# A gated cross-attention block with an expert layer: rounded queries and keys taken off ScalarE, and the last ten residuals summed by TensorE

## The chip, the cores and the metric

One Trainium2 chip, one core of it. The metric is the device time of one execution in microseconds (us); the figure given is the median of several runs. The engines are called TensorE (PE), VectorE (DVE), ScalarE (ACT), GpSimd (POOL) and SyncE (SP), as in the profile.

## The reference, cut to what matters

```python
# x, ctx: (128 batches, 64 tokens, 128 features), float32; 16 heads of 8 features
def attention(q, k, v):
    qh, kh, vh = heads(q @ W_q + b_q), heads(k @ W_k + b_k), heads(v @ W_v + b_v)
    probs = softmax(qh @ kh.T / sqrt(8))
    return merge(probs @ vh) @ W_o + b_o
x = x + tanh(g_xattn) * attention(layernorm(x), ctx, ctx)
# 8 experts 128 -> 256 -> 128, one per token, chosen by the largest gate
xn = layernorm(x)
gates = softmax((xn @ w_red) @ normalized(wg).T)
e, score = argmax(gates), max(gates)
x = x + tanh(g_ffn) * score * (gelu(xn @ W1[e] + b1[e]) @ W2[e] + b2[e])
```

## The kernel before, in words

The 8192 tokens are 64 units of 128 tokens (two batches each), and four units make a chunk: 16 chunks of 512 tokens. The attention is a pipeline over 76 slots (`SLOTS`), the outer `for k in range(SLOTS)` loop of every engine; chunk `s = k // 4` and position `j = k % 4`. In slot k TensorE computes the first scores of unit k-4 (`scores1`, called by `peaks`), the second scores of unit k-10 (`scores2`), the values of unit k-11 and the output projection of unit k-12 (`values`). Beside these, each slot holds a quarter of the preparation of chunk s: position 0 turns the normalized rows and the context, position 1 projects the keys, position 2 the queries, position 3 the values.

**Two passes over the scores.** The softmax needs the largest score of each row first. `scores1` computes scores from bfloat16 queries `qb` and keys `kb`, the latter spread by DMA into the block-diagonal tile `Kd`; VectorE reduces them to maxima (L1054, in two halves, `mxa_ok` and `mx_ok`). `scores2` computes them again in float32 from `Qd` (spread by DMA from `Qf`) and `kT`, with the maxima subtracted by a product of `MD` and `usel` (L1192). ScalarE takes the exponentials in two halves (L631, L633); the first waits for `mxa_ok` of the unit that `scores1` handled in this slot, the second for `mx_ok`. The next slot's `scores2` waits for the second exponential. So each slot closes a loop: TensorE scores2, scores1; VectorE first half of the maxima; ScalarE two exponentials; TensorE again.

**Keys and queries.** In position 1 ScalarE writes `kb` (L599, from PSUM, bias added, rounded to bfloat16) and then `kT` (L606, two instructions: float32, one for the even and one for the odd rows, each masked by `par`). TensorE's values product (L1428) overwrites the same bank `m1` and waits for both. SyncE's queue waits for `kb_ok` and issues four DMAs from `kb` to `Kd` (L325), then waits for `qf_ok` and issues four from `Qf` to `Qd` (L332), then the weight loads and the loads of later chunks. `scores1` of unit 4s runs in slot 4s+4 and waits for all four `Kd` DMAs of chunk s (L1220): three slots after `kb` is written. In position 2 ScalarE writes `qb` (L662, bfloat16) and `Qf` (L665, float32) from the same bank.

**GpSimd's queue.** For each chunk c from 2 on, `norm(c)` (called with s = c-1) computes the reciprocal deviation by a power (L380, when VectorE has the variance, L769, in slot 4(c-1)+1), three small instructions (L384, L385, L389), and then four times a normalized unit `xn` (L404) and the copy of x with the output bias (L408). TensorE turns `xn` in slot 4c. From s = 7 on GpSimd also issues the indirect DMAs that scatter finished rows to the experts' lists (`send`, L439); the table `sends` gives for each s how many stand before `norm` and how many behind it: three before at s = 8, 9, 11 and 12, four at s = 14, two at s = 15.

**Residuals.** Each unit's projected output is added to x by VectorE: `residual(k)`, L1042, `XR = out * tg + XR` over 137 columns (128 features, 8 gate logits, 1 mean). From slot 66 (`APART`) on, the output stands in a bank of its own (`m1`) and the residual is VectorE's last act for the unit in the slot; TensorE's next projection waits for it (`x1_ok`). ScalarE's `squares` (L561) read the sum a slot later. The routing (`route_peak` and what follows) runs on VectorE at slots set by `route_slots`.

**The expert layer** follows: 71 tiles of 128 rows, its first pieces inside slots 70 to 75. ScalarE loads the table of Gelu in slot 73 (L699).

## Time and profile before

| | |
|---|---|
| median of 3 runs | 354.69 us (352.94 to 355.47) |
| the profiled execution | 356.73 us |
| its span, first to last instruction | 355.0 us |
| mean granted TensorE clock | 0.968 of full speed |
| busy: PE, DVE, ACT, POOL | 300.8, 285.4, 252.8, 231.1 us |
| attention slots with scores2 | 32.55 to 240.3 us |
| expert tiles alone | from 246 us |

The page and the timeline are of the one profiled execution. A group of instructions is told by its line, the engine and the tiles it writes and reads. "[0.28 <-ACT PT L633]" behind an instruction is the idle time of its engine just before it and what ended it.

### The profile page before, as it was taken

How to read it: one execution, taken by the hardware profiler on the slowest of the kernel's cores; microseconds unless marked ns; L12 is line 12 of the kernel's file. 1: busy time of each engine (PE TensorE's matmuls, PEld its weight loads, DVE VectorE, ACT ScalarE, POOL GpSimd, SP SyncE). 2: the span in 40 equal slices, each digit the busy share in tenths (PEclk: the TensorE clock that was granted, in tenths of full speed). 3: DMA queues.
4: the chain of work that ended last, by engine and by line, in shares of the span. 5: the costliest groups of instructions: out<-in, count | busy, mean ns of one | idle time of the engine just before them, and what ended most of it. 6: DMA issues, size and time to landing. Idle time of an engine off the chain costs nothing.

```text
span 355.0 us, 16204 instructions
## 1 busy us (share of the span) xinstructions
PE 300.8 (85%) x6014; PEld 223.6 (63%) x6014; DVE 285.4 (80%) x1025; ACT 252.8 (71%) x651; POOL 231.1 (65%) x372
## 2 busy tenths in 40 slices
PE   2968899998999898999898787667988999999940
PEld 1535666665675665666665655456777999999830
DVE  7777999899998999999999799988777666666610
ACT  3766799989999889998998795767443555555410
POOL 6493654184498885798188643277777777777771
PEclk9998999999999999999999898999999999999985
DMA  5354345344313322423121112421135543433110
GB/s 118 84 172 151 92 144 175 86 142 104 96 58 122 123 67 78 143 67 118 54 74 59 67 61 75 118 71 60 49 94 141 139 118 109 110 101 101 57 41 0
DMA packets 47160, 34.05 MB, mean 96 GB/s; under 512 B 9800, under 2 KB 42955, under 8 KB 47083
## 3 DMA queue, kind: packets, MB, share of 16 engines
q1 hardware_dynamic: 42440, 23.90, 23.9%
q0 software_dynamic: 4352, 9.00, 7.6%
q8 instruction: 49, 0.80, 1.0%
q14 instruction: 27, 0.22, 0.2%
q10 hardware_dynamic: 292, 0.13, 0.1%
HBM read 17.13 MB, written 10.04 MB: 77 GB/s over the span
## 4 chain that ended last, share of the span: by engine, by line
PE 43%; DVE 22%; ACT 17%; issue 10%; POOL 3%; DMA 2%; ACTq 1%; POOLq 0%; DVEq 0%; SPq 0%
PE m L1366 10%; PE sc L1338 8%; DVE mx L1054 6%; ACT PT L633 4%; PE sc L1199 4%; ACT PT L631 3%; ACT dev L561 3%; PE sc L1209 3%; PE sc L1192 3%; PE m L1428 3%; DVE TV L1063 2%; PE m L1363 2%; PE pv L1274 2%; PE sc L1326 2%; DVE NV L1074 2%
## 5 line engine op out<-in xcount | busy, mean ns | idle before, releaser
L1054 DVE TENSOR_REDUCE mx<-sc 128x8 f32<-128x512 f32 x128 | 81.9, 682 | 14.0 <-PE sc L1209 13.7
L439 POOL DMA_INDIRECT records<-XR,pos x64 | 62.7, 979 | 35.2 <-DVE XR L926 17.5
L498 POOL DMA_INDIRECT out<-fo,rr x71 | 70.3, 990 | 21.5 <-issue 20.0
L631 ACT ACTIVATE PT<-sc 128x512 f32<-128x512 f32 x64 | 38.2, 597 | 19.1 <-issue 13.2
L380 POOL TENSOR_TENSOR rstd<-ve,mhalf 128x4 f32<-128x4 f32 x16 | 16.7, 1041 | 53.3 <-DVE ve L769 53.2
L1366 PE MATMUL m<-w,fgT 128*128 x280 | 49.0, 298 | 0.1
L1033 DVE SCALAR_TENSOR_TENSOR fo<-m,rr 128x128 f32<-128x128 f32 x70 | 24.5, 350 | 27.2 <-PE m L1366 26.9
L1338 PE MATMUL sc<-fxT,w1s 128*128 128x128 f32 x276 | 43.3, 279 | 3.1 <-DVE w1s L1025 2.7
L1274 PE MATMUL pv<-PT,V 128*32 128x64 f32 x2048 | 42.9, 223 | 1.1 <-DVE NV L1074 0.7
L614 ACT ACTIVATE fxT<-sc 128x128 f32<-128x128 f32 x69 | 19.2, 278 | 30.2 <-PE sc L1326 30.2
L1199 PE MATMUL sc<-Qd,kT 32*128 32x128 f32 x1024 | 40.3, 274 | 0.0
L1338 PEld LDWEIGHTS sc<-fxT,w1s 128*128 128x128 f32 x276 | 36.2, 191 | 5.6 <-ACT fxT L614 2.7
L620 ACT ACTIVATE fgT<-sc 128x256 f32<-128x256 f32 x69 | 26.5, 384 | 18.1 <-PE sc L1338 17.8
L633 ACT ACTIVATE PT<-sc 128x512 f32<-128x512 f32 x64 | 38.3, 598 | 0.0
L1274 PEld LDWEIGHTS pv<-PT,V 128*32 128x32 f32 x2048 | 32.3, 110 | 9.3 <-issue 2.0
L1366 PEld LDWEIGHTS m<-w,fgT 128*128 128x128 f32 x280 | 36.6, 190 | 2.2 <-issue 0.2
L1192 PEld LDWEIGHTS sc<-MD,usel 32*128 32x128 bf16 x256 | 6.4, 91 | 47.9 <-ACT PT L633 45.6
L1192 PE MATMUL sc<-MD,usel 32*128 32x256 bf16 x256 | 18.5, 280 | 21.2 <-ACT PT L633 18.9
L1199 PEld LDWEIGHTS sc<-Qd,kT 32*128 32x128 f32 x1024 | 35.1, 189 | 0.0
L1063 DVE STREAM_TRANSPOSE TV<-pv 128x256 f32<-128x256 f32 x64 | 28.2, 440 | 0.6 <-PE pv L1274 0.4
L1009 DVE TENSOR_SCALAR fx<-rr 128x127 f32<-128x127 f32 x71 | 27.9, 392 | 0.1
L561 ACT ACTIVATE dev<-XR 128x128 f32<-128x128 f32 x64 | 26.1, 407 | 0.5 <-DVE XR L1042 0.5
(229 smaller groups left out, 695.8 us busy)
## 6 DMA issues: line engine op xcount, KB each, us to landing
rr<-records SPq DMA_DIRECT2D x71, 72.0 KB, 2.0
XC<-in_x SPq DMA_DIRECT2D x16, 256.0 KB, 4.4
C<-in_ctx SPq DMA_DIRECT2D x16, 256.0 KB
Qd<-Qf SPq DMA_DIRECT2D x64, 64.0 KB
Kd<-kb SPq DMA_DIRECT2D x64, 32.0 KB, 2.2
w<-in_L_ffn_W SPq DMA_DIRECT2D x16, 128.0 KB, 3.4
out<-fo,rr POOLq DMA_INDIRECT x71, 2.3
w1l<-in_L_ffn_W SPq DMA_DIRECT2D x8, 128.0 KB, 3.9
```

The costliest lines, as they stand in the source:

```text
L439: nc.gpsimd.indirect_dma_start(out=records, out_offset=bass.IndirectOffsetOnAxis(ap=pos[:, u:u + 1], axis=0), in_=XR[:, u, :], in_offset=N ...
L498: nc.gpsimd.indirect_dma_start(out=out_rows, out_offset=bass.IndirectOffsetOnAxis(ap=rr[q][:, R_ID:R_ID + 1].bitcast(U32), axis=0), in_=fo ...
L561: nc.scalar.activation(dev2[:, :], X[:, n, :], ACT.Square, bias=XR[:, n, R_MEAN:R_MEAN + 1], scale=-1.0, accum_out=gsq[c % 2][:, u:u + 1]) ...
L631: nc.scalar.activation(pt[:, 0:2], sc[:, 0:2, 256:512], ACT.Exp)
L633: nc.scalar.activation(pt[:, 2:4], sc[:, 2:4, 256:512], ACT.Exp).then_inc(pt_ok, 1)
L1054: nc.vector.tensor_reduce(mx[c % 2][:, t:t + 2, HI * u:HI * u + HI], sc[:, t:t + 2, 0:256].rearrange("p t (i k) -> p t i k", i=HI), AX_X, ...
L1063: nc.vector.transpose(TV[:, :, :].rearrange("p a r -> p (a r)"), pv[:, 0:2 * P]).then_inc(tv_ok, 1)
L1192: nc.tensor.matmul(sc[:, t, 256:512].rearrange("p (b i q) -> p i b q", b=2, i=2), usel[r, u, :, :].rearrange("r l k -> r (l k)"), MD[c % 2 ...
L1199: m = nc.tensor.matmul(sc[:, t, 256 + P * b:256 + P * b + P].rearrange("p (i q) -> p i q", i=2), kT[c % 3][r, u, b, :, :].rearrange("r l k ...
L1274: last = nc.tensor.matmul(pv[32 * t:32 * t + 32, P * b:P * b + P].rearrange("p (h i q) -> p i h q", h=2, i=2)[:, i], vf[:, at:at + 32], PT ...
L1338: i = nc.tensor.matmul(hidden(k)[:, P * m:P * m + P], w1s[p][:, P * m:P * m + P], fxT[p][:, :], start=True, stop=True, skip_group_check=True)
L1366: i = nc.tensor.matmul(o, fgT[p][:, m, :], w2[:, bass.ds(e, 1), m, :].rearrange("p o c -> p (o c)"), start=False, stop=(m == HH - 1), skip ...
```

## The change

On ScalarE the bfloat16 queries go: `qb` becomes a view of the upper halves of the float32 `Qf` (every second bfloat16 element, cut rather than rounded), and `Qf` gets a second buffer. For chunks 2 to 15 the bfloat16 keys are no longer written by ScalarE: GpSimd adds the two halves of `kT` into `kb`, in `norm` behind `deviation`, ahead of the `xn` of the next chunk. TensorE's values product waits for `kT` alone. In the last ten slots TensorE adds x to the projected output in PSUM by a product with the identity, and ScalarE copies the sum out; `wox` is multiplied by `tg` once, so the other 54 residuals on VectorE become plain additions.

```diff
-        Qf = sb("Qf", [P, CT])
-        qb = [sb(f"qb{i}", [P, CT], BF16) for i in range(2)]
+        Qf = [sb(f"Qf{i}", [P, CT]) for i in range(2)]
+        qb = [q[:, :].bitcast(BF16).rearrange("p (t two) -> p t two", two=2)[:, :, 1] for q in Qf]
...
+            def rounded_keys(s):
+                pool.wait_ge(kT_ok, s + 1)
+                pool.wait_ge(kd_in[(s - 1) % 2], 16 * HI * ((s - 1) // 2 + 1))
+                k = kT[s % 3][:, :, :, :, :].rearrange("r u b p k -> r (u b) p k")
+                nc.gpsimd.tensor_tensor(kb[:, :].rearrange("r (a k) -> r a k", k=S), k[:, :, 0, :], k[:, :, 1, :],
+                                        ALU.add).then_inc(kb_ok, 1)
             def norm(c):
                 deviation(c)
+                if c >= 3:
+                    rounded_keys(c - 1)
...
                     norm(s + 1)
+                if s + 1 == NC:
+                    rounded_keys(s)
...
-                nc.scalar.activation(wox[:, D:DX], pv[:, 0:NX], ACT.Copy).then_inc(wox_ok, 1)
+                act.wait_ge(tg_ok, 1)
+                nc.scalar.activation(wox[:, D:DX], pv[:, 0:NX], ACT.Copy, scale=tg[:, 0:1])
+                nc.scalar.activation(wox[:, 0:D], wox[:, 0:D], ACT.Copy, scale=tg[:, 0:1]).then_inc(wox_ok, 1)
+            def residual(n):
+                act.wait_ge(pv_ps, pv_turn(n + LAGO))
+                act.wait_ge(x1_ok, n)
+                nc.scalar.activation(XR[:, n, 0:DX], attn_out(n + LAGO), ACT.Copy).then_inc(x1_ok, 1)
...
                 if j == 1 and 1 <= s < NC:
-                    keys(s)
+                    if s == 1:
+                        keys(s)
+                    else:
+                        act.wait_ge(k_ps, s + 1)
                     keys_turned(s)
                 if j == 2 and s < NC:
                     act.wait_ge(q_ps, s + 1)
                     if s >= 2:
                         act.wait_ge(s1_ps, CU * (s - 1))
-                    nc.scalar.activation(qb[s % 2][:, :], m0[:, :], ACT.Identity, bias=b16[:, 0:1], scale=ISC).then_inc(qb_ok, 1)
-                    if s >= 1:
-                        act.wait_ge(qd_in[(s - 1) % 3], 16 * HI * ((s - 1) // 3 + 1))
-                    nc.scalar.activation(Qf[:, :], m0[:, :], ACT.Identity, bias=b16[:, 0:1], scale=ISC).then_inc(qf_ok, 1)
+                        act.wait_ge(qd_in[(s - 2) % 3], 16 * HI * ((s - 2) // 3 + 1))
+                    nc.scalar.activation(Qf[s % 2][:, :], m0[:, :], ACT.Identity, bias=b16[:, 0:1], scale=ISC).then_inc(qf_ok, 1)
...
+                if APART <= k:
+                    residual(k - LAGO)
...
-                    nc.vector.scalar_tensor_tensor(out=XR[:, n, 0:DX], in0=attn_out(k), scalar=tg[:, 0:1], in1=XR[:, n, 0:DX],
-                                                   op0=ALU.mult, op1=ALU.add).then_inc(x1_ok, 1)
+                    nc.vector.tensor_tensor(XR[:, n, 0:DX], attn_out(k), XR[:, n, 0:DX], ALU.add).then_inc(x1_ok, 1)
...
-                if k >= APART:
-                    residual(k)
...
-                        pe.wait_ge(qb_ok, c + 1)
+                        pe.wait_ge(qf_ok, c + 1)
...
+                    if k >= APART:
+                        pe.wait_ge(xb_ok, no // CU + 1)
+                        pe.wait_ge(lgx_ok, no // CU + 1)
+                        nc.tensor.matmul(attn_out(k), ident[:, :], XR[:, no, 0:DX], start=True, stop=False, skip_group_check=True)
...
-                    pe.wait_ge(kb_ok, s + 1)
+                    if s < 2:
+                        pe.wait_ge(kb_ok, s + 1)
                     pe.wait_ge(kT_ok, s + 1)
```

## Rows read from the trace of the kernel before

**Rows 1.** The page, part 1: busy time of each engine, its share, its instructions.

```profile
PE 300.8 (85%) x6014; PEld 223.6 (63%) x6014; DVE 285.4 (80%) x1025; ACT 252.8 (71%) x651; POOL 231.1 (65%) x372
```

**Rows 2.** The page, part 4: the chain that ended last, by engine.

```profile
PE 43%; DVE 22%; ACT 17%; issue 10%; POOL 3%; DMA 2%; ACTq 1%; POOLq 0%; DVEq 0%; SPq 0%
```

**Rows 3.** Timeline, 136 to 144 us, PE and ACT: start us, duration us, engine, line.

```profile
136.88 0.29 PE L1192 MATMUL sc<-MD,usel 32*128 32x256 bf16 x4 [0.17 <-ACT PT L633]
...
137.33 1.44 ACT L606 ACTIVATE kT<-m,bkp,par 128x512 f32<-128x512 f32 x2
...
138.83 1.12 PE L1421 MATMUL m<-xT,wqp 128*128 128x512 f32 x2
...
139.04 0.60 ACT L631 ACTIVATE PT<-sc 128x512 f32<-128x512 f32 x1
...
140.18 0.29 PE L1192 MATMUL sc<-MD,usel 32*128 32x256 bf16 x4 [0.22 <-ACT PT L633]
...
143.21 0.29 PE L1192 MATMUL sc<-MD,usel 32*128 32x256 bf16 x4
```

**Rows 4.** Lines by form: line, engine, shapes, count | busy us, mean ns | idle.

```profile
L1209 PEld LDWEIGHTS sc<-Kd,qb 32*64 32x64 bf16 x512 | 8.0, 102 | 8.7 <-DVE mx L1054 1.3 <-issue 0.2
...
L423 POOL TENSOR_TENSOR w<-w,w1l 128x512 f32<-128x512 f32 x4 | 5.0, 1284 | 0.0
...
L599 ACT ACTIVATE kb<-m,b 128x512 bf16<-128x512 f32 x16 | 11.0, 686 | 2.0 <-PE m L1316 2.0
...
L1042 DVE SCALAR_TENSOR_TENSOR XR<-m,tg,XR 128x137 f32<-128x137 f32 x10 | 3.2, 324 | 0.0
```

**Rows 5.** Timeline, 137 to 142 us, POOL and SP's queue.

```profile
137.31 1.04 POOL L380 TENSOR_TENSOR rstd<-ve,mhalf 128x4 f32<-128x4 f32 x1 [5.41 <-DVE ve L769]
...
137.46 2.39 SPq L325 DMA_DIRECT2D Kd<-kb  x4
...
138.86 0.19 POOL L389 TENSOR_TENSOR std<-ve,rstd 128x4 f32<-128x4 f32 x1
```

**Rows 6.** The tile Kd: issue ns min/median/max and landing us, whole run; landing, 137 to 141 us.

```profile
L325 SPq DMA_DIRECT2D Kd<-kb x64: 459/592/1567, 12.2 to 208.0; - x64
...
DMA to landing us min/median/max: 1.6/2.2/3.6
...
DMA to landing us min/median/max: 1.7/1.8/1.8
```

**Rows 7.** Timeline, 143 to 146 us: the slot that first uses these keys.

```profile
143.88 0.32 PE L1209 MATMUL sc<-Kd,qb 32*64 32x256 bf16 x8
...
144.29 1.29 DVE L1054 TENSOR_REDUCE mx<-sc 128x8 f32<-128x512 f32 x2 [0.26 <-PE sc L1209]
...
145.32 0.58 ACT L631 ACTIVATE PT<-sc 128x512 f32<-128x512 f32 x1
```

**Rows 8.** Timeline, 111 to 118, 151 to 157 and 191 to 199 us: three other chunks.

```profile
111.83 1.06 POOL L380 TENSOR_TENSOR rstd<-ve,mhalf 128x4 f32<-128x4 f32 x1
...
116.94 0.32 PE L1209 MATMUL sc<-Kd,qb 32*64 32x256 bf16 x8
...
117.99 0.68 DVE L1054 TENSOR_REDUCE mx<-sc 128x8 f32<-128x512 f32 x1
...
151.38 1.05 POOL L380 TENSOR_TENSOR rstd<-ve,mhalf 128x4 f32<-128x4 f32 x1
...
156.48 0.32 PE L1209 MATMUL sc<-Kd,qb 32*64 32x256 bf16 x8
...
191.61 1.06 POOL L380 TENSOR_TENSOR rstd<-ve,mhalf 128x4 f32<-128x4 f32 x1
...
198.75 0.32 PE L1209 MATMUL sc<-Kd,qb 32*64 32x256 bf16 x8
```

**Rows 9.** Windows: stretch us, span, busy us of PE, PEld, DVE, ACT, POOL, PEclk, DMA.

```profile
200.00:203.00 3.00, 3.00 (x30) 2.62 (x30) 1.90 (x7) 2.71 (x7) 1.58 (x2) 0.52 0.19 64
```

**Rows 10.** Timeline, 241 to 243 us, ACT: the table load of the last exponentials.

```profile
241.71 1.28 ACT L699 ACT_TABLE_LOAD   x1
```

More of the change, by code:

```diff
@@ L189, in gated_block @@
         q_ps, k_ps, v_ps = (sem(n) for n in ("q_ps", "k_ps", "v_ps"))
-        qb_ok, qf_ok, kb_ok, kT_ok, v_ok = (sem(n) for n in ("qb_ok", "qf_ok", "kb_ok", "kT_ok", "v_ok"))
+        qf_ok, kb_ok, kT_ok, v_ok = (sem(n) for n in ("qf_ok", "kb_ok", "kT_ok", "v_ok"))
         kd_in = [sem(f"kd_in{i}") for i in range(2)]
@@ L331, in _ @@
                 for i in range(HI):
-                    sp.dma_start(Qd[s % 3][i::HI, i // 2, :], Qf[i::HI, :]).then_inc(qd_in[s % 3], 16)
+                    sp.dma_start(Qd[s % 3][i::HI, i // 2, :], Qf[s % 2][i::HI, :]).then_inc(qd_in[s % 3], 16)
                 if s == 0:
@@ L597, in keys @@
                 if s >= 1:
-                    act.wait_ge(kd_in[(s - 1) % 2], 16 * HI * ((s - 1) // 2 + 1))
+                    act.wait_ge(kd_in[0], 16 * HI)
                 nc.scalar.activation(kb[:, :], m1[:, :], ACT.Identity, bias=b16[:, 1:2]).then_inc(kb_ok, 1)
@@ L1287, in values @@
                         q = slice(32 * t, 32 * t + 32)
-                        last = nc.tensor.matmul(attn_out(k)[q, :], OT[no % 2][:, q], wox[:, :], start=True, stop=True,
+                        last = nc.tensor.matmul(attn_out(k)[q, :], OT[no % 2][:, q], wox[:, :], start=k < APART, stop=True,
                                                 skip_group_check=True)
```

## The prediction, made before the change was run

> **What bounds the kernel now.** I read the page first: PE is busy 85% of the span, DVE 80%, ACT 71% [rows 1], and the chain that ended last is PE 43%, DVE 22%, ACT 17% [rows 2]. POOL has 3% of it and the DMAs 2%. So three engines hand the end to each other, and shares can't price the change; the slot has to be read. In the timeline a slot is the distance between two starts of L1192. Undisturbed it is 143.21 - 140.18 = 3.03 us [rows 3]: the loop scores2, scores1, first half of the maxima, two exponentials. The slot before took 3.30: there ACT was still at kT until 138.77 (after kb) and then at the squares, so the first exponential started only at 139.04 [rows 3]. That is the only slot of the four in a chunk that kb lengthens. PE in it ends its query projection at 139.95 [rows 3], 3.07 us after the slot began, so PE allows little less.
>
> Then I looked for what waits for kb. SP issues the four Kd DMAs at 137.46 in 2.39 us [rows 5]. The last one, some 0.59 us long, therefore starts at 139.26, and lands 1.8 us later in this chunk [rows 6], at 141.1. scores1 of this chunk's first unit starts at 143.88 [rows 7]. The keys have 2.8 us to spare here. Over the whole run a landing takes 1.6 to 3.6 us, median 2.2, and an issue up to 1.57 us [rows 6]: from first issue to last landing 1.8 + 2.2 = 4.0 us as a rule, and 1.0 more where one issue is long. I take 4.4. The usual spare is then 143.88 - 137.46 - 4.4 = 2.0 us.
>
> **ScalarE without kb and qb.** Each was 16 instructions of about 0.686 us, 11.0 us together [rows 4] (the row is of kb; qb has its shape and operation); 14 kb and 16 qb go, 20.6 us of ACT's busy time. On the path: in the slot with kb the excess over the floor, 3.30 - 3.07 = 0.23 us, in each of 13 chunks, 3.0 us at most. qb lies in a slot that takes 3.03 already [rows 3], with PE, DVE and the loop beside it: nothing. Qf comes 0.69 us earlier, which nobody needs. The second Qf buffer removes a wait that ended nobody's idle time: nothing.
>
> **GpSimd makes kb.** The price of the new instruction: POOL's 128x512 addition of two tiles in SBUF, L423, takes 1.284 us [rows 4]. That is the same size and operand count; float32 output instead of bfloat16. Bounds: as ACT's 0.69 [rows 4], and 1.28 twice if the conversion or runs of 64 elements cost. I take 1.28, the nearest row. The Trainium skill, "GPSIMD Engine Reference", Instruction dispatch, counts about 2.5 cycles per element at 1.2 GHz for two inputs, an estimate of 1.07 us for 512 elements; with that every lateness below would shrink by 0.2 us. The row is slower than the page, and the row has the instruction's start in it.
>
> What matters more is its place. It stands behind L380 and the three small ones. In the chunk of rows 5 L380 waits for the variance until 137.31 and L389 ends at 139.05, later than kT (138.77 [rows 3], 0.69 earlier without kb). So kb is ready at 139.05 + 1.28 = 140.33 in place of 137.46: 2.9 us later. Against a usual spare of 2.0 the keys are 0.9 us late for scores1 (with this chunk's own quick landings 0.1). PE issues in order: behind the waiting scores1 stand the values, the output projection and the turns of xn, and DVE's maxima and ACT's exponentials wait for it, so the slot grows. The cover: the first half of the maxima ended at 144.29 + 0.65 = 144.94, while ACT started the exponential at 145.32 [rows 7]; up to 0.38 us is hidden, and I take 0.3 because PE's own work in that slot moves too. Net 0.6 us in each of nine chunks (3, 4, 6, 7, 9, 10, 12, 13 and, weaker, 2): 5.4 us. Bounds 0 (all land as in rows 6's second stretch) and 1.6 each (one long issue): 0 to 14 us. Chunk 5 is covered by a late reduction. And where the keys set the time, the 0.23 us above is not gained: it only brings the deadline forward.
>
> Three chunks are worse, because there POOL is saturated by sends ahead of norm. There L380 starts with no idle before it: 111.83, 151.38 and 191.61 [rows 8]; the 1.28 us that the previous chunk's addition put into the queue shifts it too. From L380's start to kb I count 1.06 + 0.7 (three small ones, 138.35 to 139.05 [rows 5]) + 1.28, plus that 1.28: 4.3 us; then 4.4 to the last landing.
> - Chunk 8: 111.83 + 8.7 = 120.5; scores1 started at 116.94 [rows 8]: 3.6 late. DVE's reduction there began at 117.99, 0.7 behind the end of scores1 [rows 8], which hides that much and the 0.3 beside it: 2.7.
> - Chunk 11: 151.38 + 8.7 = 160.1 against 156.48: 3.6 late, 3.3 net.
> - Chunk 14: 191.61 + 8.7 = 200.3 against 198.75: 1.6 late, 1.3 net.
> Together 7.3 us, bounds 4 (landings as in chunk 10, 0.8 quicker each, and half the shift) and 12.
>
> xn comes 1.3 us later (2.6 in those three); PE turns it behind the same scores1, so it stays hidden. Qd is issued behind Kd and is needed six slots later: nothing. The loads of x and context behind them have several us: nothing. The ACT gain stays where Kd does not bind, chunk 15 and parts of 12 and 10: -0.5.
>
> **A clock term.** In 200 to 203 us the granted clock is 0.52, that is 1.2 GHz for nearly all of it, and PE is busy through it [rows 9]; it followed a slot in which PE idled. Stalls of 3 us may bring more such stretches; one costs about 1 us. None is in the sum as new; up to three are in the range.
>
> **The strided queries.** Loading qb took 102 ns for 64 columns [rows 4]. Read at every second element it may take as long (0) or twice that; eight loads on four row groups could then add 0.05 to 0.1 us to scores1, on the loop, in 64 slots: 0 to 6 us. No row shows a strided load. I take 0, since loads overlap the products. The Trainium skill, "SBUF — State Buffer", Door 1: The DMA port swizzle, in its box on cachelines, says that bfloat16 may be strided up to eight elements at no loss; by it the term is 0 as well.
>
> **The last ten residuals.** DVE loses ten instructions of 0.324 us [rows 4]; three or four of them lie on DVE's stretch of the chain: -1.1. ACT gains ten copies of about 0.3 (137 columns; bounds 0.28 and 0.6); in most slots ACT idles, but in slot 68 it is the bound, and in slot 73 the copy stands ahead of the Gelu table load that takes 1.28 us at 241.71 [rows 10]: +0.6. PE's ten identity products of 0.3 us lie in its waits for the exponentials, except the last two or so. Net -0.5, bounds -1.5 and +1.5. Scaling wox is two ACT instructions once, 0 to 0.5; the plain additions on DVE save nothing I can price (0 to -0.03 each, 54 of them).
>
> **Sum.** 5.4 + 7.3 - 0.5 - 0.5 = +11.7 us. The profiled execution goes from 356.73 (span 355.0) to 368.4; it stood 2.0 above the median, so the median goes from 354.69 to 366.4.
>
> **Rivals.**
> - Faster: the keys arrive in time after all. It needs kb's way on POOL plus the four landings to fit in 6.4 us (143.88 - 137.46), and POOL's backlog to be absorbed. Then 13 x 0.23 and the tail's 0.5 to 1.5 are gained: 354.7 - 3.5 - 0.5 = about 351. For it: ACT's 20 us less, and ACT holds 17% of the chain. Against: the spare is 2.0 and the shift 2.9, and in the three saturated chunks 5.7. It decides once the shift is below 2. Chance 0.12.
> - Partly: regular chunks just in time (landings at 1.8, as in chunk 10), only the three saturated ones late: 354.7 + 7.3 - 10 x 0.23 - 0.5 = 359.2. Chance 0.2.
> - No more than noise, gains and stalls of one size: 0.06.
> - Worse: the addition takes twice as long, or strided loads or the low clock come on top. Nine regular chunks with 1.3 more are 11.7 us; strided loads at their upper end or three low stretches 3 to 6. About 372 to 378. Chance 0.14.
> - The forecast itself, 362 to 371: 0.48. The Trainium skill, "SBUF — State Buffer", Who interferes with whom, adds one in the same direction: a VectorE instruction with two SBUF inputs is blocked while a GpSimd instruction reads SBUF. Here routing instructions would wait up to the addition's length in five groups; that is inside the forecast's own range.
>
> A measurement of this kernel tells about 1% from no change, 3.5 us. Faster by more: 0.12; within: 0.06; slower: 0.82. The range 356.5 to 375.
>
> **What would show it.** In the profile after: PE waiting at L1209 for the DMA of Kd, once in nearly every chunk and longest at chunks 8, 11 and 14; the distance of L1192 starts 3.07 in the old 3.30 slots; the addition at 1.3 us between L389 and L404; POOL's idle ahead of L380 smaller by 1.3; fewer DVE us before 242. It is wrong if L1209 never waits for a DMA, if the addition lies far from 1.3 us, or if the time is lost in the last ten slots.

## The result, and the profile after

| | before | after |
|---|---|---|
| median | 355.08 us (352.94 to 356.96) | 372.65 us (372.12 to 373.33) |
| span of the profiled execution | 355.0 us | 369.6 us |
| mean granted clock | 0.968 | 0.964 |
| first scores2 | 32.55 us | 31.66 us |

The ratio is 1.0486, 95% interval 1.0442 to 1.0529, from four runs of each. The forecast was 366.4, +11.7 us; it came to 372.65, +17.6 in the medians and 369.6 - 355.0 = +14.6 in the spans. One of the experiments below, loads_behind, had two of its four runs disturbed, so it has no ratio and is read by its profiled execution.

The page of after, part 1 (busy time of each engine, against [rows 1]) and part 4 (the chain that ended last, against [rows 2]):

```profile
PE 307.6 (83%) x6034; PEld 228.9 (62%) x6034; DVE 283.5 (77%) x1015; ACT 241.5 (65%) x632; POOL 247.8 (67%) x386
...
PE 48%; DVE 21%; issue 14%; ACT 9%; SPq 2%; POOL 2%; DMA 1%; POOLq 0%; DVEq 0%; ACTq 0%
```

ACT lost 11.3 us of busy time and POOL gained 16.7. The instructions that left ACT add up to 20.6 us and those that came to 3.3 (2.8 for the ten copies of XR, the rest for `wox`); the busy time fell by less, since ACT's instructions overlap in the trace and an overlap counts once. ACT went from 17% of the chain to 9%, and what took its place is PE and "issue": time in which an engine waited for nothing that the profile shows. The groups by form say on which instructions:

```profile
L1228 PE MATMUL sc<-Kd,Qf 32*64 32x256 bf16 x512 | 20.6, 298 | 12.4 <-issue 10.7 <-DVE mx L1075 1.8
L1228 PEld LDWEIGHTS sc<-Kd,Qf 32*64 32x64 bf16 x512 | 8.4, 103 | 20.6 <-issue 12.6 <-DVE mx L1075 2.2
...
L404 POOL TENSOR_TENSOR kb<-kT 128x512 bf16<-128x512 f32 x14 | 17.7, 1267 | 5.1 <-ACT kT L625 5.1
...
L1064 DVE TENSOR_TENSOR XR<-pv,XR 128x137 f32<-128x137 f32 x54 | 14.3, 265 | 0.0
...
L606 ACT ACTIVATE XR<-m 128x137 f32<-128x137 f32 x10 | 2.8, 285 | 1.5 <-PE m L1311 1.5
...
L925 DVE TENSOR_TENSOR ky<-ky,oh 128x64 f32<-128x64 f32 x2 | 1.4, 704 | 0.0
```

L1228 is the scores1 of after (L1209 before). Its weight loads stood idle 20.6 us, against 8.7 before [rows 4], and 12.6 of them are "issue". These are the late keys, and in part the low clock and the holes told of below. The profile does not name the DMA of Kd as the releaser; that it is the DMA shows only when each wait is laid beside a landing.

Chunk 10, the chunk whose rows the prediction used. Timeline of after, 145 to 155 us: start, duration, engine, line, [idle before <-what ended it].

```profile
145.56 1.04 POOL L380 TENSOR_TENSOR rstd<-ve,mhalf 128x4 f32<-128x4 f32 x1 [4.47 <-DVE ve L791]
...
147.10 0.19 POOL L389 TENSOR_TENSOR std<-ve,rstd 128x4 f32<-128x4 f32 x1
...
147.25 1.26 POOL L404 TENSOR_TENSOR kb<-kT 128x512 bf16<-128x512 f32 x1
...
148.54 3.42 SPq L325 DMA_DIRECT2D Kd<-kb  x4
...
151.43 0.29 PE L1211 MATMUL sc<-MD,usel 32*128 32x256 bf16 x4 [0.15 <-ACT PT L652]
...
153.24 0.32 PE L1228 MATMUL sc<-Kd,Qf 32*64 32x256 bf16 x8 [1.07 <-issue]
...
154.40 0.60 ACT L650 ACTIVATE PT<-sc 128x512 f32<-128x512 f32 x1 [0.77 <-DVE mx L1075]
```

And the tile Kd, 148 to 152.5 us, on SP's queue (issue durations in ns, then first and last start in us):

```profile
L325 SPq DMA_DIRECT2D Kd<-kb x4: 465/590/1633, 148.5 to 151.4; - x4
...
DMA to landing us min/median/max: 1.8/2.3/2.9
```

The last of the four DMAs starts at 151.37 and lands 1.8 us later, at 153.15. scores1 starts at 153.24, 0.09 us behind. Without the wait it would have started 0.67 us after its scores2, as before (143.88 - 143.21, [rows 3, 7]): at 152.10. So the keys are 1.14 us late here, and the slot is 4.19 us where it was 3.23.

Chunk 8, one of the three with POOL saturated by sends, timeline 117 to 129 us:

```profile
117.33 0.96 POOL L449 DMA_INDIRECT records<-XR,pos  x1 [0.30 <-issue]
118.31 1.05 POOL L380 TENSOR_TENSOR rstd<-ve,mhalf 128x4 f32<-128x4 f32 x1
...
120.01 1.27 POOL L404 TENSOR_TENSOR kb<-kT 128x512 bf16<-128x512 f32 x1
...
121.30 2.38 SPq L325 DMA_DIRECT2D Kd<-kb  x4
...
122.02 0.29 PE L1211 MATMUL sc<-MD,usel 32*128 32x256 bf16 x4
...
124.95 0.44 PE L1228 MATMUL sc<-Kd,Qf 32*64 32x256 bf16 x8 [2.19 <-issue]
...
125.32 1.08 PE L1293 MATMUL pv<-PT,V 128*32 128x64 f32 x32
...
128.73 0.29 PE L1211 MATMUL sc<-MD,usel 32*128 32x256 bf16 x4
```

L380 has no idle before it: the send ahead of it ended as it began. The last landing was at 124.86, and scores1 again started 0.09 us behind it, 124.95 - (122.02 + 0.67) = 2.26 us late. It was 0.09 us behind the last landing in chunks 4 and 6 too. Chunk 11 was 2.77 us late; in the regular chunks 4, 5, 6, 7, 9, 10 and 13 the lateness was 0.5 to 1.1 us, and the keys of chunks 2, 3, 12 and 14 were not late.

**A low clock behind the waits.** The values product L1293 took 1.08 us behind the late scores1, where it takes 0.65 in other slots. Windows of after: stretch us, span, busy us of PE, PEld, DVE, ACT, POOL, PEclk, DMA.

```profile
53.50:56.50 3.00, 3.00 (x76) 2.44 (x78) 1.50 (x7) 1.84 (x5) 0.00 (x0) 0.50 0.29 96
125.00:128.00 3.00, 3.00 (x54) 2.36 (x55) 2.36 (x8) 1.21 (x3) 2.52 (x4) 0.50 0.28 101
169.50:172.50 3.00, 3.00 (x30) 2.67 (x29) 2.68 (x12) 2.74 (x7) 2.22 (x3) 0.50 0.32 103
214.00:217.00 3.00, 3.00 (x29) 2.41 (x23) 2.11 (x8) 2.63 (x7) 1.82 (x2) 0.50 0.23 79
```

The granted clock is 0.50, which is 1.2 GHz, in four stretches between the first scores2 and slot 66. Before had two there, one of them in [rows 9], the other from 217 us. Ahead of each of the four PE had just stood still: 2.5 us in slot 15 (the hole told of below), 2.2 and 2.7 us for the keys of chunks 8 and 11, and 3.5 us in slot 59. What it costs is an estimate from the other key slots: from a late scores1 to the next scores2 took 2.35 to 2.38 us in slots 28, 32, 40, 44 and 56, but 3.78 in slot 36 and 3.39 in slot 48. That is 1.4 and 1.0 us. Slot 16, whose keys were in time (their last DMA began at 50.16, scores1 at 55.25), grew by 1.0. Together about 3.5 us of the key slots' growth is the clock.

**Where the span's 14.6 us are.** A slot is the distance between two starts of scores2, as in the prediction; slot 4c + 4 is the one in which the keys of chunk c are first used. The sums over slots, in us:

| stretch | before | after | difference | forecast |
|---|---|---|---|---|
| up to the first scores2 | 32.55 | 31.66 | -0.9 | 0 |
| nine regular key slots (16, 20, 24, 28, 32, 40, 44, 52, 56; the forecast's nine had 12 in place of 24) | 30.48 | 34.82 | +4.3 | +5.4 |
| three saturated key slots (36, 48, 60) | 11.23 | 17.90 | +6.7 | +7.3 |
| slots 15 and 23, where PE stands still | 6.07 | 10.58 | +4.5 | none |
| slot 59, where DVE is blocked | 4.83 | 6.35 | +1.5 | none as a term |
| 13 slots in which ScalarE wrote kb (14, 18, ... 62) | | | -1.4 | 0 to -0.5 |
| all other slots to 65 | | | +0.9 | 0 |
| slot 66 to the end | | | -1.0 | -0.5 |
| sum | | | +14.6 | +11.7 |

The two key groups together: forecast 12.7, measured 11.0, of which about 3.5 is the low clock and 7.5 the late keys themselves. Outside them, what was missed lies in slots 15, 23 and 59, 6.0 us together.

**The holes in PE.** Slot 15, timeline of after, 49.3 to 53 us:

```profile
49.42 0.28 PE L1311 MATMUL pv<-wox,OT 128*32 128x137 f32 x1
...
52.23 0.44 PE L1311 MATMUL pv<-wox,OT 128*32 128x137 f32 x7 [2.53 <-issue]
...
52.73 0.45 DVE L1084 STREAM_TRANSPOSE TV<-pv 128x256 f32<-128x256 f32 x1 [2.35 <-PE pv L1311]
```

L1311 is one output projection: eight records of 32 columns in a row (four calls in the kernel), with no wait between the first and the second. PE stood still inside it until 52.23, for 2.75 us by its weight loads (from 49.48) and 2.53 by its products. Slot 23 has one of 1.65 us inside the values product L1293 (78.03 to 79.69). In the trace of before no gap inside a product is over 0.4 us from the first scores2 on. What else went on then, the DMA view of 48 to 53 us and the load of XC issued ahead of it:

```profile
DMA packets 1605, 0.90 MB, mean 179 GB/s; under 512 B 135, under 2 KB 1571, under 8 KB 1603
...
q8 instruction: 1, 0.02, 1.4%
q14 instruction: 1, 0.01, 0.4%
```

```profile
L264 SPq DMA_DIRECT2D XC<-in_x x1: 452/452/452, 45.3 to 45.3; - x1
...
DMA to landing us min/median/max: 6.9/6.9/6.9
```

A load that takes 4.5 us as a median over the run took 6.9 and landed at 52.23, the moment at which PE went on. Two packets on the instruction queues start at 49.59 and 52.23; the first, of 16 KB on q8, ended at 50.72. In before the packet in this place started at 47.53, and PE came to this product at 50.2. This looks like a fetch of PE's next instructions that waits behind row loads; the experiments below bear on it.

**Slot 59.** Timeline of after, 206 to 212 us:

```profile
206.36 1.27 POOL L404 TENSOR_TENSOR kb<-kT 128x512 bf16<-128x512 f32 x1
206.50 1.23 DVE L925 TENSOR_TENSOR ky<-ky,oh 128x64 f32<-128x64 f32 x1
...
208.87 0.50 DVE L955 TENSOR_TENSOR tl<-tl 128x6 f32<-128x6 f32 x1
...
209.72 0.50 DVE L955 TENSOR_TENSOR tl<-tl 128x4 f32<-128x4 f32 x1
...
210.26 1.29 DVE L1075 TENSOR_REDUCE mx<-sc 128x8 f32<-128x512 f32 x2
...
211.03 0.60 ACT L650 ACTIVATE PT<-sc 128x512 f32<-128x512 f32 x1 [4.24 <-issue]
```

The same place in before, 191 to 199 us:

```profile
193.92 0.37 DVE L903 TENSOR_TENSOR ky<-ky,oh 128x64 f32<-128x64 f32 x1
...
195.21 0.34 DVE L933 TENSOR_TENSOR tl<-tl 128x6 f32<-128x6 f32 x1
```

The routing product L925 (64 columns, two inputs in SBUF) ends when the GpSimd addition does, and took 1.23 us where it had taken 0.37. Behind it stand six small operations on `tl`, the last of which ran beside GpSimd's xn instructions in both traces; they took 1.55 us in all in before and 2.28 here, where more of them ended with one of GpSimd's. Then come the maxima that the exponential waits for. So 0.9 us are lost to the product and 0.7 to the small ones, in a slot that DVE already set.

### The profile page after: what moved, and what is told of

It reads as the page before. It is cut to its first block, busy times and chain, and to the rows that moved or that the text cites. A ratio compares the mean times of both kernels' runs of the same rounds, so it can differ in the third digit from the quotient of the medians.

```text
span 369.6 us, 16228 instructions
## 1 busy us (share of the span) xinstructions
PE 307.6 (83%) x6034; PEld 228.9 (62%) x6034; DVE 283.5 (77%) x1015; ACT 241.5 (65%) x632; POOL 247.8 (67%) x386
## 4 chain that ended last, share of the span: by engine, by line
PE 48%; DVE 21%; issue 14%; ACT 9%; SPq 2%; POOL 2%; DMA 1%; POOLq 0%; DVEq 0%; ACTq 0%
PE m L1389 10%; PE sc L1361 8%; PE sc L1218 5%; DVE mx L1075 5%; PE pv L1293 4%; ACT PT L650 4%; ACT PT L652 3%; PE sc L1211 3%; PE sc L1228 3%; PE pv L1311 2%; PE m L1426 2%; PE m L1386 2%; DVE TV L1084 2%; PE sc L1349 2%; PE m L1332 2%
## 5 line engine op out<-in xcount | busy, mean ns | idle before, releaser
L1075 DVE TENSOR_REDUCE mx<-sc 128x8 f32<-128x512 f32 x128 | 82.0, 682 | 24.9 <-PE sc L1228 24.2
L380 POOL TENSOR_TENSOR rstd<-ve,mhalf 128x4 f32<-128x4 f32 x16 | 16.6, 1040 | 51.9 <-DVE ve L791 51.8
L1293 PE MATMUL pv<-PT,V 128*32 128x64 f32 x2048 | 43.5, 225 | 1.7 <-issue 1.6
L1293 PEld LDWEIGHTS pv<-PT,V 128*32 128x32 f32 x2048 | 32.7, 111 | 10.0 <-issue 2.9
L1211 PE MATMUL sc<-MD,usel 32*128 32x256 bf16 x256 | 18.8, 283 | 18.4 <-ACT PT L652 16.7
L1228 PE MATMUL sc<-Kd,Qf 32*64 32x256 bf16 x512 | 20.6, 298 | 12.4 <-issue 10.7
```

What stands on the lines that cost most here:

```text
L1075: nc.vector.tensor_reduce(mx[c % 2][:, t:t + 2, HI * u:HI * u + HI], sc[:, t:t + 2, 0:256].rearrange("p t (i k) -> p t i k", i=HI), AX_X, ...
L1211: nc.tensor.matmul(sc[:, t, 256:512].rearrange("p (b i q) -> p i b q", b=2, i=2), usel[r, u, :, :].rearrange("r l k -> r (l k)"), MD[c % 2 ...
L1228: m = nc.tensor.matmul(sc[o, t, 0:256].rearrange("p (i k) -> p i k", i=HI), qb[c % 2][r, tokens(n, b)], Kd[c % 2][r, :, tokens(n, b)], sta ...
L1293: last = nc.tensor.matmul(pv[32 * t:32 * t + 32, P * b:P * b + P].rearrange("p (h i q) -> p i h q", h=2, i=2)[:, i], vf[:, at:at + 32], PT ...
```

## The experiments

Theory L is that of the prediction: the path of kb through GpSimd brings the keys too late. Rivals: H, that TensorE holes from instruction fetches are a cost of their own; P, that GpSimd's reading blocks VectorE; and that the queries or the residuals cost something. Here "kernel before" is the one at hand on the same chip (356.22, 355.64 or 355.89 us).

| run | median us | ratio to before, 95% | span us |
|---|---|---|---|
| keys_back | 353.32 | 0.9957 (0.9912 to 1.0002) | 351.4 |
| keys_only | 374.95 | 1.0537 (1.0459 to 1.0614) | 371.9 |
| tail_only | 354.15 | 0.9942 (0.9916 to 0.9968) | 351.2 |
| queries_only | 356.18 | 1.0004 (0.9968 to 1.0039) | 354.5 |
| keys_first | 364.53 | 1.0207 (1.0114 to 1.0300) | 364.5 |
| sends_behind | 366.62 | 1.0290 (1.0198 to 1.0383) | 362.2 |
| first_and_behind | 362.82 | 1.0161 (1.0071 to 1.0252) | 360.9 |
| add_twice | 386.22 | 1.0828 (1.0681 to 1.0975) | 381.4 |
| loads_behind | 370.73 | none | 365.3 |
| all_three | 361.51 | 1.0174 (1.0111 to 1.0236) | 358.9 |
| fill_instead | 371.01 | 1.0422 (1.0353 to 1.0492) | 368.2 |
| keys_back_5 | 354.20 | 0.9941 (0.9905 to 0.9977) | 354.7 |

### Taking the change apart

keys_back: the kernel after, with ScalarE writing kb in every chunk again. Queries and residuals stay changed.

```diff
             def norm(c):
                 deviation(c)
-                if c >= 3:
-                    rounded_keys(c - 1)
...
-                    if s == 1:
-                        keys(s)
-                    else:
-                        act.wait_ge(k_ps, s + 1)
+                    keys(s)
...
-                    if s < 2:
-                        pe.wait_ge(kb_ok, s + 1)
+                    pe.wait_ge(kb_ok, s + 1)
```

> The changed kernel with ScalarE writing the rounded keys of all chunks again; the cut queries and the moved residuals stay. Theory L (late keys: GpSimd's addition makes the Kd transfers land after scores1 wants them, and its reads block VectorE): all of the loss goes, 353 to 355.5 us, and scores1 waits for no transfer. Rival Q (the strided queries and the copies and identity products in the last slots cost the time): 365 to 372 us.

353.32 us: everything lost comes back. The weight loads of scores1 in its trace, by form, are at 9.3 us of idle, with VectorE's maxima and not "issue" as its largest part:

```profile
L1213 PEld LDWEIGHTS sc<-Kd,Qf 32*64 32x64 bf16 x512 | 8.2, 104 | 9.3 <-DVE mx L1060 2.0
```

keys_only: the kernel before, with only the keys moved to GpSimd (the same lines the other way round).

```diff
             def norm(c):
                 deviation(c)
+                if c >= 3:
+                    rounded_keys(c - 1)
```

> The kernel before with only the keys moved to GpSimd. Theory L: 371 to 375 us, about the changed kernel plus the 1 us that its last slots gain. Rival Q: 354 to 358 us.

374.95 us; its span is 16.9 over before: regular key slots +5.5, saturated +6.6, slots 15 and 23 +3.8, slot 59 +1.8. The holes are there too, at 50.9 to 53.44 and 79.33 to 80.86 us, inside the same two products. So both late keys and holes come with this one edit.

tail_only: the kernel before, with only the residuals changed (two places of the edit).

```diff
+                if APART <= k:
+                    residual(k - LAGO)
...
-                    nc.vector.scalar_tensor_tensor(out=XR[:, n, 0:DX], in0=attn_out(k), scalar=tg[:, 0:1], in1=XR[:, n, 0:DX],
-                                                   op0=ALU.mult, op1=ALU.add).then_inc(x1_ok, 1)
+                    nc.vector.tensor_tensor(XR[:, n, 0:DX], attn_out(k), XR[:, n, 0:DX], ALU.add).then_inc(x1_ok, 1)
```

> The kernel before with only the residuals changed (last ten in PSUM, the others plain additions, wox scaled once). Theory L: 353 to 355 us, since the trace of the changed kernel shows about 1 us less after slot 65. Rival Q: 358 us or more.

354.15 us, ratio 0.9942: 2 us faster than before. Its span is 3.8 us shorter: -1.3 from slot 66 on and -2.3 in slots outside every group of the table. But some of the latter is the choice of the profiled executions: slot 51 gives 0.7 of it, and is as much shorter in queries_only, which left the residuals alone. So where the 2 us lie isn't shown. Its residual group by form:

```profile
L1052 DVE TENSOR_TENSOR XR<-pv,XR 128x137 f32<-128x137 f32 x54 | 14.2, 263 | 0.0
```

The same 54 took 17.3 us in the old form, 0.320 each: 0.06 less, 54 times, 3.1 us of VectorE. The run changed these and the last ten together and doesn't tell what each is worth.

queries_only: the kernel before, with only the strided view of Qf and its second buffer.

```diff
-        Qf = sb("Qf", [P, CT])
-        qb = [sb(f"qb{i}", [P, CT], BF16) for i in range(2)]
+        Qf = [sb(f"Qf{i}", [P, CT]) for i in range(2)]
+        qb = [q[:, :].bitcast(BF16).rearrange("p (t two) -> p t two", two=2)[:, :, 1] for q in Qf]
```

> The kernel before with only the queries changed (a strided view of Qf in two buffers). Theory L: 354 to 356 us, ScalarE's 11 us lie beside other work and the strided weight loads cost nothing (they take 0.12 us for eight in both traces). Rival Q: 358 to 361 us, 0.05 to 0.1 us for each of 64 slots.

1.0004: nothing, as forecast. The strided weight load takes 103 ns, the packed one took 102 [rows 4].

keys_back_5: keys_back again, run more often, to see whether it beats before.

```diff
             def norm(c):
                 deviation(c)
-                if c >= 3:
-                    rounded_keys(c - 1)
```

> The same kernel as keys_back (only the queries and the residuals changed), timed in more rounds to see whether it beats the kernel before: 352.5 to 355 us, ratio 0.992 to 0.998, no better than the residuals alone (0.994), since the queries alone gave 1.000.

0.9941 (0.9905 to 0.9977): faster by about 2 us, the same as tail_only (0.9942). The residuals account for all of the gain; that ScalarE is rid of 16 query instructions adds nothing to it that can be told.

### When the keys are ready

keys_first: the addition stands ahead of the three small operations and the wait for the variance.

```diff
             def norm(c):
-                deviation(c)
                 if c >= 3:
                     rounded_keys(c - 1)
+                deviation(c)
```

> The changed kernel with GpSimd's addition ahead of the deviation instead of behind it: kb then waits for kT alone and is ready about 0.85 us earlier in chunks where GpSimd is idle, 1.75 us earlier in the three where it is saturated. Theory L (the landing of Kd sets scores1): 9 x 0.6 to 0.8 plus 3 x 1.7 less, 360 to 364 us. Rival R (GpSimd's load as such, or blocking of VectorE, costs the time, wherever the addition stands): 370 us or more.

Chunk 10 in its trace, POOL, SP's queue and PE, 144.5 to 151 us:

```profile
144.57 1.26 POOL L404 TENSOR_TENSOR kb<-kT 128x512 bf16<-128x512 f32 x1 [4.26 <-ACT kT L625]
145.81 1.04 POOL L380 TENSOR_TENSOR rstd<-ve,mhalf 128x4 f32<-128x4 f32 x1
145.87 3.50 SPq L325 DMA_DIRECT2D Kd<-kb  x4
```

The addition now follows kT at once. 364.53 us, 8 less than after and just outside what was expected. Regular key slots fell from +4.3 to +2.5. The saturated ones fell only from +6.7 to +5.7: slot 36 is still 6.56 us, since there the sends ahead of norm, not the order inside it, set the time, and a low-clock stretch follows, from 122.9 us on, as in after. Slots 15 and 23 grew to 12.6 us together, holes of 2.74 and 1.93.

sends_behind: the order of norm as in after; in six steps the sends ahead of norm go behind it.

```diff
-        sends = {7: (0, 3), 8: (3, 1), 9: (3, 2), 10: (0, 4), 11: (3, 2), 12: (3, 0), 13: (0, 4), 14: (4, 2), 15: (2, 8), 16: (0, 0),
+        sends = {7: (0, 3), 8: (0, 4), 9: (0, 5), 10: (0, 4), 11: (0, 5), 12: (0, 3), 13: (0, 4), 14: (0, 6), 15: (0, 10), 16: (0, 0),
                  17: (4, 4), 18: (0, 4)}
```

> The changed kernel with all indirect DMAs of a step behind norm instead of partly ahead of it (the same number per step). Theory L: chunks 8 and 11 lose their extra lateness (about 2.7 us each), chunk 14 nothing or 1 us since VectorE sets it: 366 to 368.5 us. Rival R: within 1 us of 372.65.

366.62 us, as expected. Above all the saturated group goes, from +6.7 to +0.6, and the regular one mostly stays (+3.3): the two halves of the lateness are separate, as the prediction had them. With the long waits at chunks 8 and 11 the low-clock stretches behind them went too (none between 35 and 222 us), so some 2.4 of the 6.1 us are the clock.

first_and_behind: both edits together.

```diff
             def norm(c):
-                deviation(c)
                 if c >= 3:
                     rounded_keys(c - 1)
+                deviation(c)
...
-        sends = {7: (0, 3), 8: (3, 1), 9: (3, 2), 10: (0, 4), 11: (3, 2), 12: (3, 0), 13: (0, 4), 14: (4, 2), 15: (2, 8), 16: (0, 0),
+        sends = {7: (0, 3), 8: (0, 4), 9: (0, 5), 10: (0, 4), 11: (0, 5), 12: (0, 3), 13: (0, 4), 14: (0, 6), 15: (0, 10), 16: (0, 0),
```

> Both edits: addition ahead of the deviation, sends behind norm. Theory L: nearly all lateness gone, the slots with kb at 3.07 instead of 3.30 remain gained, what stays is VectorE blocked by GpSimd's reads and TensorE's two holes: 355 to 361 us. Rival R: 368 us or more.

362.82 us, a miss: 5.9 us of the span remain. Saturated -0.3 and slot 59 +0.1 are mended; +3.7 stay in the regular key slots and +3.3 in slots 15 and 23. Of the +3.7, 2.5 are no late keys: slot 16 (+1.2) runs at the low clock behind the hole of slot 15, and in slot 24 (+1.3) scores1 was in time and the maxima stood behind this pair (timelines of 82 to 85 us, POOL and DVE):

```profile
82.47 2.52 POOL L433 TENSOR_TENSOR w<-w,w1l 128x512 f32<-128x512 f32 x2
...
82.44 2.67 DVE L889 TENSOR_TENSOR ex<-XR,clog 128x96 f32<-128x96 f32 x1
```

It is the collision of slot 59 with another neighbour, a VectorE product that takes 0.43 us in chunk 8 of after; in before it took 1.08 in slot 24. In other chunks the keys are still late, by up to 1.3 us. Its scores1 loads, by form, still wait 6 us longer than before:

```profile
L1228 PEld LDWEIGHTS sc<-Kd,Qf 32*64 32x64 bf16 x512 | 8.7, 104 | 14.7 <-issue 6.6 <-DVE mx L1075 1.9
```

Even at its earliest the addition doesn't beat ScalarE's: it starts behind kT, which ScalarE itself now writes first, and takes 1.27 us against 0.69.

add_twice: in each chunk a second addition of the same size, into an unused tile `kb2`, ahead of the real one.

```diff
                 k = kT[s % 3][:, :, :, :, :].rearrange("r u b p k -> r (u b) p k")
+                nc.gpsimd.tensor_tensor(kb2[:, :].rearrange("r (a k) -> r a k", k=S), k[:, :, 0, :], k[:, :, 1, :], ALU.add)
                 nc.gpsimd.tensor_tensor(kb[:, :].rearrange("r (a k) -> r a k", k=S), k[:, :, 0, :], k[:, :, 1, :],
```

> The changed kernel with a second addition of the same size ahead of the one that makes kb, written to a tile that nobody reads: kb 1.28 us later in each chunk, 2.6 in the saturated ones. Theory L: 10 to 13 chunks pass it on in full, 385 to 393 us. Rival R': the lateness is mostly covered and the loss lies elsewhere: below 378 us.

386.22 us, within what was expected. The loads of scores1:

```profile
L1229 PEld LDWEIGHTS sc<-Kd,Qf 32*64 32x64 bf16 x512 | 8.6, 105 | 32.3 <-issue 24.9 <-DVE mx L1076 2.2
```

Their "issue" doubled from 12.6 to 24.9 us. The slots of chunk 8 and chunk 11 went from 6.7 and 6.8 to 8.7 and 9.1, +2.0 and +2.3, somewhat under two additions (the chunk's own and the one queued before it). Nothing but GpSimd's work ahead of kb was changed, and the span grew by 381.4 - 369.6 = 11.8 us for 14 times 1.27. The key slots alone grew by as much (regular +7.6, saturated +4.2; the rest cancels), slot 59 by 0.6: the keys set the time, not GpSimd's load as such. The low-clock stretches behind longer waits are part of it, as above.

### The holes

loads_behind: the loads of x and context of steps 3 and 5, those that run while PE stands still, are issued behind Kd and Qd.

```diff
             for s in range(NC):
-                if s:
+                if s not in (0, 3, 5):
                     next_loads(s)
...
-                if s == 0:
+                if s in (0, 3, 5):
                     next_loads(s)
```

> The changed kernel with the loads of x and context of steps 3 and 5 issued behind that step's Kd and Qd transfers instead of ahead of them. Theory H (TensorE's two holes, 2.75 us at 49.5 and 1.65 us at 78.0, are instruction fetches that queue behind a burst of row loads, which late keys push onto them): both holes gone from the trace, 3 to 4.5 us less, 368 to 369.5 us, unless the moved burst meets another fetch. Rival: the holes stand where they stood, 372 to 373 us.

The profiled execution took 368.1 us, span 365.3, where after had 369.6. The hole in slot 15 is gone and that of slot 23 is 0.83 us in place of 1.65: slots 15 and 23 together +0.9, not +4.5. The regular key slots rose a little (+5.5). This supports the row loads' part in the holes, though the second hole was expected to go too.

all_three: first_and_behind with loads_behind (the line of `sends` as there, not shown again).

```diff
-                if s:
+                if s not in (0, 3, 5):
                     next_loads(s)
...
             def norm(c):
-                deviation(c)
                 if c >= 3:
                     rounded_keys(c - 1)
+                deviation(c)
```

> Addition ahead of the deviation, sends behind norm, and the two row loads behind Kd and Qd. Theory L with H: 362.8 less the 3.6 us of its two holes, 358 to 360.5 us. Rival: 362 to 364 us.

361.51 us, a miss by 1 us, just above what was expected. It is 1.3 below first_and_behind, but against the kernel before the two can't be told apart (1.0174 and 1.0161, with intervals that overlap). Slots 15 and 23 fell to +0.4, but two new holes came, 1.16 us at 63.96 and 1.06 at 90.08, in steps whose loads were not moved. The fetch seems to meet the loads elsewhere rather than not at all.

How far the holes are settled: they are at the same two instructions in after, keys_only, keys_first, sends_behind, first_and_behind and fill_instead (1.4 to 2.7 us); in add_twice (0.5 and 1.4) and tail_only (0.4 and 0.7) they are smaller; queries_only has one of 0.6 at 78.7; keys_back has none, and the same kernel as keys_back_5 has one of 1.24 us at 74.05. They move when loads move. So they depend on the timing of loads against PE, not on the new instruction as such. That an instruction fetch is what waits is borne out by the packets on q8, 16 KB each, 49 or 50 in a run: taking the holes of 0.6 us or more in the weight loads of all traces, 19 of them, each ended 1.2 to 1.6 us after the end of such a packet. It is still not shown, since no run took the fetch away.

### GpSimd and VectorE

fill_instead: in the place of the addition GpSimd fills an unused tile in the same time. The rounded keys of chunks 2 to 15 are left out, so their maxima come from older keys.

```diff
-                k = kT[s % 3][:, :, :, :, :].rearrange("r u b p k -> r (u b) p k")
-                nc.gpsimd.tensor_tensor(kb[:, :].rearrange("r (a k) -> r a k", k=S), k[:, :, 0, :], k[:, :, 1, :],
-                                        ALU.add).then_inc(kb_ok, 1)
+                nc.gpsimd.memset(scratch[:, :], 0.0).then_inc(kb_ok, 1)
```

> The changed kernel with GpSimd's addition replaced by a fill of 1420 float32 elements of an unused tile, as long (about 1.28 us, from 1.80 us for 2048 and 0.54 for 512), at the same place; the rounded keys of chunks 2 to 15 are left out, so their maxima come from the keys of chunk 1, and only the shift of the exponentials changes. A fill reads nothing. Theory P (VectorE's instructions with two SBUF inputs are blocked while GpSimd reads; 1.5 us at slot 59): the product of places and one-hots in slot 58 falls from 1.23 to 0.4 us and slot 59 to about 4.9 us; total 370.5 to 371.5 us, with the late keys unchanged. Rival: blocking by any GpSimd instruction, or another cause: 1.23 us stays, 372 to 373 us.

Its timeline, 206 to 211 us:

```profile
206.07 0.18 DVE L923 TENSOR_TENSOR ky<-ky,oh 128x64 f32<-128x64 f32 x1
206.26 1.27 POOL L403 MEMSET scratch<- 128x1420 f32 x1
206.43 1.15 DVE L988 COPY tl<-tl 128x8 f32<-128x8 f32 x1
...
209.73 1.29 DVE L1073 TENSOR_REDUCE mx<-sc 128x8 f32<-128x512 f32 x2
```

371.01 us: the total is what was expected, the mechanism was not. The two-input product escaped this time, being over before the fill began, and took 0.18 us; but the little copy behind it, 8 columns, took 1.15 us and ended with the fill. Slot 59 stayed at 6.25 us (after: 6.35, before: 4.83). So the 1.5 us of slot 59 are a collision of DVE with GpSimd, seen in both traces, and it didn't need GpSimd to read: here a fill was enough to hold a copy. It goes when GpSimd's instructions stand elsewhere: slot 59 is +0.1 in first_and_behind, where the addition is over by then. In keys_first it is +0.1 too, though the product was held as long (timeline of 202 to 205 us):

```profile
202.45 1.13 DVE L925 TENSOR_TENSOR ky<-ky,oh 128x64 f32<-128x64 f32 x1
```

There the reciprocal deviation runs behind the addition, not xn, and the six small operations took 0.96 us in place of 2.28. So the place of xn's instructions matters here no less than that of the addition.

## Why the prediction was right, and where it was short

The direction, the main mechanism (keys that land too late) and the range (356.5 to 375) held. That the total came as near as it did is in part luck: the late keys by themselves cost about 7.5 us where 12.7 were forecast, and the low clock, the holes in PE and slot 59, all at nothing in the sum, cost about 3.5, 4.5 and 1.5. Step by step:

- **The addition's price**, forecast 1.28 us from the nearest row [rows 4], measured 1.267. The estimate from the Trainium skill's "GPSIMD Engine Reference", Instruction dispatch, 1.07 us, was too low by 0.2; the trace decides.
- **Its place.** kb was to be ready 2.9 us later. Counted from the scores2 of its slot it was ready at 137.46 - 136.88 = 0.58 us before [rows 3, 5] and at 148.51 - 145.19 = 3.32 after: 2.74 later. Right.
- **The path of the DMAs.** 4.4 us were taken; chunk 10 took 153.15 - 148.54 = 4.6, with one issue of 1.6, and chunk 8 124.86 - 121.30 = 3.6. The bounds held, and the mean was fair.
- **Nine regular chunks**, 0.6 each. Four grew by more (slots 16, 28, 32, 44: 1.02, 0.83, 0.84, 0.96), slot 56 by 0.48, slot 20 by 0.3 and three by nothing: chunk 9 was 0.9 late and covered, chunk 12 was in time, chunk 5 (24) was covered as said. Slot 16 is the clock and not the keys. Chunk 2 (slot 12) didn't grow. +4.3 for 5.4, and 3.3 without slot 16.
- **Three saturated chunks.** 3.6 late was said for chunk 8; 2.26 came, 0.8 of the difference because the four landings took 3.6 and not 4.4. But behind the late scores1 PE worked in one run to the next scores2, most of it at half its clock (124.95 to 128.73, 3.78 us where 2.4 is usual), so the slot grew by 3.03, part of it borrowed from the next (3.72 to 3.17). Chunk 11 was 2.77 late and grew by 3.6 for 3.3, 1.0 of it the clock. That these two sums came out is luck. Chunk 14 grew by 0.05 for 1.3: slot 59 had grown already, and the keys landed 1.2 us ahead of their use. +6.7 for 7.3.
- **The slots that ScalarE's kb lengthened.** The other 12 gained 0.2 each, 2.4 us, slot 62 lost 1.0. The forecast took 0.5 in all, holding that a gain only brings the deadline of the keys forward. The term was mis-sized by 0.9 us, in the same direction as the two above: all three made the forecast too high, 2.6 us together, and what the sum lacked hid it.
- **The strided queries and Qf's buffer**: nothing, right twice (queries_only, and 103 ns a load).
- **The last ten residuals**: -1.0 in the slots from 66 on, -1.3 in tail_only, for -0.5. In the same part stands a step that was mis-sized: "the plain additions on DVE save nothing I can price". It allowed 0 to 0.03 us each; they take 0.06 us less each, and tail_only, which has both edits, is 2 us faster than before.
- **The clock term** was priced rightly, about 1 us a stretch (1.0, 1.4 and 1.0 here), and counted wrongly: none was in the sum, and after has four where before had two.
- **What the sum lacked** is what made it short. Slots 15 and 23, +4.5 us: no step of the prediction looked at PE standing still with no wait, for in the trace of before nothing like it is to be seen. And slot 59, +1.5: the prediction had the collision of the product, 0.9 of it, and called it "inside the forecast's own range" in place of asking on which of the five groups DVE sets the slot. Slot 59 was at 4.83 us, the longest of all; there a micro-second on DVE is one on the end.
- **The rivals.** That the keys arrive in time, or late in three chunks only, fell with add_twice and sends_behind. "Worse" gave 372 to 378 and 372.65 is in it, and for one of its reasons: the addition didn't take twice as long and strided loads cost nothing, but the low clock came on top. The figure given for "Faster" subtracts 3.5 where 13 times 0.23 is 3.0; about 351 stands either way.

The distance between the span's +14.6 and the medians' +17.6 is mostly the choice of the two executions: that of before (356.73 us) stood 1.6 above the median of its runs, that of after (372.13) 0.5 below its own, and what lies around the span grew from 1.7 to 2.5 us. What stays open is what makes the holes, and in which slots the residuals' gain lies.

## What to carry to other kernels

Work that is moved to an idle engine is priced by when its result is ready, not by how busy its old engine was: here 20.6 us of instructions were taken off ScalarE, and the result came 2.7 us later at a consumer that had 2.0 to spare, behind four serial DMAs. Count from the new producer's queue to the consumer in the most crowded stretch of each engine, and look there too for neighbours that hold each other up. Where a long wait comes onto PE, look whether a low clock follows it: the four longest here were each followed by one. And run a change's parts by themselves: the only edit that paid was the residuals', which has a simpler VectorE form that had been priced at nothing.

## What the runs showed of the hardware that was not expected

- PE stood still inside a chain of products, with no semaphore to wait for, 1.4 to 2.75 us, in the first case while a 256 KB row load was in flight that took 6.9 us in place of 4.5 to land. Each such hole ended 1.2 to 1.6 us after the end of a 16 KB packet on the instruction queue q8. Moving two of the loads took the hole of slot 15 away and brought smaller ones elsewhere.
- A two-input VectorE product of 128x64, 0.18 us by itself (fill_instead) and 0.37 in before, took 1.23 us beside a GpSimd addition that reads SBUF, and a copy of 128x8 elements, 0.21 us in after, took 1.15 beside a GpSimd fill. The Trainium skill, "SBUF — State Buffer", Who interferes with whom, has the first, and says of copies that they can enter a mode in which they contend with GpSimd; the traces of after and fill_instead agree.
- After PE had stood still for 2.2 to 3.5 us in slots 15, 36, 48 and 59, the granted clock was 0.50 in the windows from 53.5, 125, 169.5 and 214 us, and a values product there took 1.08 us in place of 0.65.
- An addition of PSUM and SBUF, 128x137 elements, takes VectorE 263 ns as a plain tensor_tensor and 320 to 324 as a scalar_tensor_tensor.
- A weight load of 64 bfloat16 columns read at every second element takes 103 ns, packed 102.
